# Building the token table on chip, and moving the next batch's convolution ahead

## The reference

```python
x = _layernorm(x + attention(x))                  # chunked linear attention, 16 heads, rotary, decay per head
x = _layernorm(x + selective_scan(ctx, z=x))      # per token: state = state * exp(dt * A) + dt * u * B ; y = sum(state * C)
x = _layernorm(x + experts(x))                    # 64 experts, top 8 per token, capacity 256
```

```python
probs = softmax(x @ router_weight.T)              # 2048 tokens, 64 experts
topw, topi = top_k(probs, 8);  topw /= sum(topw)
pos = (cumsum(one_hot(topi.reshape(-1))) at the chosen expert) - 1
xe[expert, pos] = x[token]   where pos < 256      # the rest is dropped
y = sum over the 8 choices of topw * expert(xe)[expert, pos]
```

## Time and profile before

| | us |
|---|---|
| median of 3 runs (1345.42 to 1348.79) | 1347.47 |
| the profiled execution | 1349.46 |
| its span, first to last instruction | 1347.6 |

### The profile page before, as it was taken

One profiled execution on the slowest core, in us unless ns is written; L12 is line 12 of the kernel. 1 busy time (PEld: TensorE's weight loads), 2 busy tenths in 40 slices (PEclk: granted clock), 3 DMA queues, 4 the chain that ended last, 5 costly groups with the idle time before them and its releaser, 6 DMA issues. The chain is left out here.

```text
span 1347.6 us, 19321 instructions
## 1 busy us (share of the span) xinstructions
PE 1138.9 (85%) x6389; PEld 757.4 (56%) x6389; DVE 1100.1 (82%) x1536; ACT 853.8 (63%) x1536; POOL 1003.9 (74%) x796
## 2 busy tenths in 40 slices
PE   7489997898979779967887718999999999999950
PEld 2234443354424434433443418999999999999940
DVE  2379988989968799878798566998888989898846
ACT  5474585734756444847345326888878888888843
POOL 0778768777899997999988744777777777777644
PEclk9698887997889789878978658999999999999985
DMA  6525425323242432163133306999999999999978
GB/s 244 140 72 191 110 65 145 99 70 83 49 111 61 124 84 51 46 154 106 38 83 102 98 13 208 302 315 305 308 304 306 305 313 301 313 301 311 285 138 326
DMA packets 97490, 235.26 MB, mean 175 GB/s; under 512 B 20704, under 2 KB 21216, under 8 KB 96752
## 3 DMA queue, kind: packets, MB, share of 16 engines
q1 hardware_dynamic: 65648, 162.66, 39.5%
q0 software_dynamic: 31744, 71.37, 22.3%
HBM read 147.48 MB, written 52.94 MB: 149 GB/s over the span
## 5 line engine op out<-in xcount | busy, mean ns | idle before, releaser
L1226 DVE TENSOR_TENSOR_SCAN hst<-hst,dbu 128x512 f32<-128x512 f32 x256 | 299.2, 1214 | 97.1 <-POOL dbu L1035 71.8
L1035 POOL TENSOR_TENSOR dbu<-rep,bc 128x1024 f32<-128x1024 f32 x128 | 301.8, 2360 | 64.1 <-PE y_ps L396 35.3
L1642 POOL DMA_INDIRECT sum_rows<-ye,tokens x128 | 205.5, 1606 | 98.4 <-ACT ye L1721 75.6
L396 PE MATMUL y_ps<-dbu,cs 128*32 128x512 f32 x512 | 167.8, 741 | 70.3 <-DVE dbu L1232 62.6
L799 ACT ACTIVATE hst<-rep,small_sb 128x512 f32<-128x512 f32 x256 | 165.9, 685 | 56.8 <-DVE dbu L1232 51.5
L1634 POOL DMA_INDIRECT xe<-x_rows,tokens x128 | 150.6, 1176 | 61.4 <-issue 37.8
L434 PE MATMUL ring<-first_raw,xT 128*128 128x512 f32 x384 | 176.7, 604 | 0.5 <-DVE x2T L1314 0.5
L1232 DVE TENSOR_TENSOR dbu<-hst,bc 128x1024 f32<-128x1024 f32 x128 | 156.7, 1224 | 4.4
L1684 PE MATMUL low<-xh,w1h 128*128 128x256 f32 x512 | 150.5, 294 | 0.0
L1684 PE MATMUL low<-xh,w1l 128*128 128x256 f32 x512 | 145.3, 284 | 0.0
L1684 PE MATMUL low<-xl,w1h 128*128 128x256 f32 x512 | 145.2, 284 | 0.0
(11 more groups left out here) (198 smaller groups left out, 2680.0 us busy)
## 6 DMA issues: line engine op xcount, KB each, us to landing
first_raw<-in_gate_up SPq DMA_DIRECT2D x64, 768.0 KB, 9.8
rep<-made SPq DMA_DIRECT2D x256, 128.0 KB
second_raw<-in_down SPq DMA_DIRECT2D x64, 256.0 KB, 5.1
bc<-bc_rows SPq DMA_DIRECT2D x64, 128.0 KB, 3.2
second_raw<-in_down SPq DMA_DIRECT2D x64, 128.0 KB, 7.2
rows<-sum_rows SPq DMA_DIRECT2D x16, 512.0 KB, 8.9
sum_rows<-x2T SPq DMA_DIRECT2D x1, 4608.0 KB, 17.2
xT<-in_x_turned SPq DMA_DIRECT2D x16, 256.0 KB, 3.0
```

Of the source, the lines that this page charges most:

```text
L396: ins = pe.matmul(y_ps[rows, :], sel, dbu[:, n % WORK, g, :], start=(k == 0), stop=(k == QUADS - 1))
L1035: pool.tensor_tensor(dbu[:, n % WORK, :, :], rep[:, i % 2, :, 1, :], bc[:, k, 0, :].unsqueeze(1).broadcast_to([P, 2, T]), ALU.mult).then_i ...
L1226: dve.tensor_tensor_scan(h, h, dbu[:, n % WORK, i, :], 0.0, ALU.mult, ALU.add).then_inc(scanned, 1)
L1642: pool.indirect_dma_start(sum_dram[e % SUMS], bass.IndirectOffsetOnAxis(ap=tokens[:, e, j:j + 1], axis=0), ye[:, e % YE, j, :], None, comp ...
```

## The change

The DRAM table, POOL's scatters, and batch 3's split into 16 x 16 go. Instead every batch has its slot numbers split into a row 0 to 127 (`slot >> 7`) and a column 0 to 127 (`slot & 127`), by `number_slots`. For 128 tokens (a pair r, j: batch and quarter) DVE makes two one-hots of 128 x 8 columns in f16, one for the rows and one for the columns (`make_hots`), ACT multiplies the second by the token's number plus one (`number_lows`), PE multiplies them in eight matmuls, one for each of the eight choices (`place_tokens`), and DVE adds the 128 x 128 result to the table in SBUF (`add_slots`). The first three batches do that in the loop, at the slots of `HOTS`: one-hots at slot n, numbering and matmuls two slots later, the addition three slots later. The counter that the one-hots are compared with is read with a step of zero in the loop (`count16`), and from a written-out copy (`count8`) for the last batch. That one follows behind the loop (`place_last`), which then fills empty slots with spare row numbers and writes `tokens`; this is before the change of block.

```diff
+HOT_AT = ((0, 3, 1), (0, 3, 4), (1, 0, 1), (1, 0, 4))
+HOT_LAST = ((0, 2, 1), (0, 2, 4), (0, 3, 0), (0, 3, 3))
+HOTS = {SLOT_COUNT * (r + 1 + over) + UNIT * c + k: (r, j)
+        for r in range(B - 1) for j, (over, c, k) in enumerate(HOT_LAST if r == B - 2 else HOT_AT)}
+def hots_due(n, later=0):
+    return (HOTS[n - later],) if n - later in HOTS else ()
+def hot_place(j):
+    return 1 if j < 2 else 0
...
+        hot = acc[...].bitcast(F16).rearrange("p (i h s k) -> p i h s k", i=2, h=2, k=TOPK)
+        hot_last = bc[...].bitcast(F16).rearrange("p (j h s k) -> p j h s k", j=NT, h=2, k=TOPK)
+        count8 = xT[:, 0, :, :]...bitcast(F16).rearrange("p (s k) -> p s k", k=TOPK)
...
+            def place_tokens(r, j):                                             # PE
+                pe.wait_ge(lows_numbered, NT * r + j + 1)
+                ps = to_fill(pe, f"slots{r}_{j}")
+                for k in range(TOPK):
+                    ins = pe.matmul(ps[:, 0:P], hot[:, hot_place(j), 1, :, k], hot[:, hot_place(j), 0, :, k],
+                                    start=(k == 0), stop=(k == TOPK - 1))
+                ins.then_inc(fill_sem(f"slots{r}_{j}"), 1)
...
+            def number_lows(r, j, lows):                                        # ACT
+                act.wait_ge(hots_made, NT * r + j + 1)
+                act.activation(lows, lows, ACT.Copy, scale=cs[:, C_TOK + NT * r + j:C_TOK + NT * r + j + 1])\
+                    .then_inc(lows_numbered, 1)
...
-            def scatter(b, first, end):                                         # POOL
-                for n in range(min(first, NT * TOPK), min(end, NT * TOPK)):
-                    pool.indirect_dma_start(table_dram, ... idx_s[:, n:n + 1] ..., tok_i[...], None)
...
-            def tell_slots(b, own):                                             # DVE
+            def number_slots(b, own):
                 own.settle()
+                own.step(dve.tensor_scalar(slot_i[:, 0, :, :], idxf[:, :, :], float(P - 1), None, ALU.add))
+                own.settle()
+                own.step(dve.tensor_scalar(slot_i[:, 1, :, :], slot_i[:, 0, :, :], 7, None, ALU.arith_shift_right))
+                own.step(dve.tensor_scalar(slot_i[:, 2, :, :], slot_i[:, 0, :, :], P - 1, None, ALU.bitwise_and))
+                own.settle()
+                own.step(dve.tensor_scalar(place_of[:, 0, :, :], slot_i[:, 1, :, :], -1.0, None, ALU.add))
+                dve.tensor_copy(place_of[:, 1, :, :], slot_i[:, 2, :, :]).then_inc(placed, 1)
+            def add_slots(r, j):
+                use = f"slots{r}_{j}"
+                ps = full(dve, use)
+                dve.tensor_tensor(tokens_f, ps[:, 0:P].rearrange("p (e j) -> p e j", j=CJ), tokens_f, ALU.add)\
+                    .then_inc(drain_sem(use), 1)
+            def make_hots(r, j, hots, count):
+                dve.wait_ge(placed, r + 1)
+                for h in range(2):
+                    ins = dve.tensor_tensor(hots[:, h, :, :], place_of[:, h, j, :].unsqueeze(1).broadcast_to([P, P, TOPK]),
+                                            count, ALU.is_equal)
+                ins.then_inc(hots_made, 1)
+            def number_tokens(r, j):
+                ...                                 # waits until the place in acc is free
+                make_hots(r, j, hot[:, hot_place(j)], count16[:, :].unsqueeze(2).broadcast_to([P, P, TOPK]))
+            def place_last(own):
+                for j in range(NT):
+                    make_hots(B - 1, j, hot_last[:, j], count8)
+                ps = full(dve, f"slots{B - 1}")
+                ...                                 # add, find empty slots, write tokens: three passes
```

The orders of the engines change with it. A line here names the place of a piece before and after (c, k as above; "k" is the slot behind whose decays, product or scan it stands):

```diff
 DVE   convolve(b + 1, 0..3)                 -c 2, k 2, 3, 4, 5            +c 2, k 0, 1, 2, 3
 PE    project_context(b + 1, 0..3)          -c 2, k 0, 1, 2, 3            +c 1, k 7 and c 2, k 0, 1, 2
 PE    project_u(b + 1)                      -c 2, k 6                     +c 2, k 5
 PE    turn_rows(b - 1, 0..1)                -in rate_experts              +ahead of update_state, mix_values
 PE    count_places(b - 1)                   -c 1, k 4                     +c 1, k 5
 ACT   first_tap(b + 1, 0..3)                -c 2, k 3, 4, 5, 6            +c 2, k 1, 2, 3, 4
 ACT   gate_u(b + 1)                         -c 2, k 7                     +c 2, k 5
 ACT   take(xdbl), soften, exponentials      -c 3, k 1, 2, 3               +c 2, k 7; c 3, k 1, 2
 ACT   logs(b + 1, EARLY)                    -c 3, k 4, with the rounding  +c 3, k 3; rounded: c 3, k 4
 ACT   logs(b, LATE)                         -c 0, k 6, with the rounding  +c 0, k 6; rounded: c 0, k 7
 ACT   exponents(b - 1)                      -c 1, k 5                     +c 1, k 4
 ACT   take_rows(b - 1, 0..3)                -c 1, k 3, 3, 4, 4            +c 1, k 2, 2, 3, 4
 ACT   gate_z(b, 2)                          -c 3, k 2                     +next batch's c 0, k 2 (last batch as before)
 ACT   excess, steps (b, 2..3)               -c 0, k 7 and c 1, k 3        +c 1, k 1 to 4
 POOL  soft_parts, soft_rest(b + 1, 0)       -c 3, k 4, 5                  +c 3, k 3, 4
 POOL  steps_of_u(b + 1, 0)                  -c 3, k 6, before inputs      +c 3, k 5, before rotate
 POOL  soft_rest(b + 1, 1)                   -c 3, k 7                     +next batch's c 0, k 0
 POOL  soft_parts(b, 2..3)                   -c 0, k 6, 7                  +c 0, k 7; c 1, k 0
 POOL  soft_parts(0, 1) before the loop      -before steps_of_u(0, 0)      +behind rotate(0)
 SP    load_context(b + 1)                   -c 1, k 6                     +c 1, k 4
 SP    store_rows(b + 1)                     -c 3, k 1                     +c 3, k 0
```

More of the change, by code:

```diff
@@ L802, in first_tap @@
             def first_tap(b, m):
-                if m == 0:
-                    wait(act, routed, b - 1)
+                if b >= 3 and m < 2:
+                    full(act, f"slots{b - 3}_{NT - 1}")
                 if m == 0 and b == 0:
@@ L818, in soften @@
             def soften(b, tiles):
+                if tiles == LATE and b >= 2:
+                    full(act, f"slots{b - 2}_1")
                 for m in tiles:
@@ L919, in _ @@
                     decays(n + 1)
+                    for r, j in hots_due(n + 1, 2):
+                        number_lows(r, j, hot[:, hot_place(j), 1, :, :])
+                    if front:
+                        first_tap(b + 1, 0)
                     if soft:
-                        act.wait_ge(bc_stored, 16 * (b + 1))
-                        take(f"xdbl{b + 1}", xdbl[:, :])
+                        soften(b + 1, EARLY)
+                    if c == 0 and b:
+                        excess(b, 1)
+                        steps(b, 1)
+                    if c == 1:
+                        excess(b, 2)
                     if back and c == 1:
@@ L927, in _ @@
                     decays(n + 2)
+                    for r, j in hots_due(n + 2, 2):
+                        number_lows(r, j, hot[:, hot_place(j), 1, :, :])
+                    if front:
+                        first_tap(b + 1, 1)
                     if soft:
-                        soften(b + 1, EARLY)
+                        exponentials(b + 1, EARLY)
                     if t:
@@ L936, in _ @@
                         gate_z(b, 1)
-                    if c == 3:
+                    if c == 3 and last:
                         gate_z(b, 2)
-                    decays(n + 3)
-                    if front:
-                        first_tap(b + 1, 0)
-                    if soft:
-                        exponentials(b + 1, EARLY)
-                    if c == 1:
-                        for m in LATE:
-                            steps(b, m)
-                    take_mixed(t)
                     if back and c == 1:
@@ L1158, in _ @@
                         n = SLOT_COUNT * b + UNIT * c + k
-                        if c == NT - 1 and k == 6 and not last:
-                            steps_of_u(b + 1, 0)
                         if n + 1 < SLOT_COUNT * B:
@@ L1194, in _ @@
-                        if k == 5 and t + 1 < NT * B:
-                            rotate(t + 1)
-                        if k in (6, 7) and c == 0:
-                            soft_parts(b, k - 4)
+                        if k == 0 and c == 0 and b:
+                            soft_rest(b, 1)
+                            steps_of_u(b, 1)
+                        if k == 7 and c == 0:
+                            soft_parts(b, 2)
+                        if k == 0 and c == 1:
+                            soft_parts(b, 3)
```

414 lines of the change are left out of this document (194 added, 220 removed).

## The result

The kernel after the change takes 1379.68 us (median of 4 runs, 1377.47 to 1381.78) against 1346.73 us for the kernel before (4 runs): the ratio is 1.0243, 95% interval 1.0221 to 1.0265. It is 2.4% slower. The forecast was 1331 us, faster. The profiled execution of the kernel after is 1381.78 us long, its span 1379.5, 2.1 us above the median.

A forecast was written before the change was run, and what follows sets the result against it. VectorE was taken to bound the loop (busy 607.14 of 704.30 us). From the profiled 1349.5 us, loop -8.6 and join -7.7 gave 1333.2; less 2.0 for the profile against the median: 1331 us, range 1315 to 1349.

The forecast's parts named there:

- scatters leave GpSimd: Loop: the 96 indirect stores leave GpSimd, and the time they cost goes: -22 us.
- the rounding: Loop, chunk 0: ScalarE's rounding passes come after the next decays, so decay stalls shrink: -1.5 us in each of four batches.
- the join: After the loop, from the places to the first gather: 24.1 us before the change, -7.7 us in sum.
- both lie two slots behind the one-hots: Loop: ScalarE's numbering (1.1 us) and TensorE's eight matmuls (1.0 us) run beside scans and cost nothing.
- If that cover is gone: Loop: should numbering and matmuls not be hidden beside scans, the price is 1.1 us twelve times, 13.
- The convolution's passes move: Loop, chunk 2: passes go from slots 2-5 to 0-3, costing 0, or 1.5 us a batch if accompanying work is late.
- the contention: Loop: VectorE's one-hots and GpSimd's instructions hinder each other: +10 us, 0.4 us per one-hot.
- Rival A: Loop: one-hots wait for GpSimd and hold up its next product, 1.6 us each: 1359 us in all; chance 0.12.
- the cover: Loop, mostly chunk 3: one-hots and additions fit into waits that VectorE already has: -13 us.
- the exponentials' wait: Loop, routing: ScalarE's exponentials come one slot sooner, and VectorE's wait for them goes: -7.5 us over three batches.
- the reordered prologue: Before the loop: `steps_of_u` comes ahead of `soft_parts`, which leaves the way of the load of `wo`: -1.6 us.
- Rival B: Loop: the waits only move, so the moves' 14.5 us are lost: 1345.5 us, no change; chance 0.12.

The follow-up runs named there:

- a_no_place: Kernel after, with TensorE's placing matmuls and VectorE's additions of the first three batches left out, one-hots and numbering kept: 1349.70 us.
- a_k_major: Kernel after, with the loop's one-hots laid out choice by choice, so that the placing matmuls read neighbouring words: 1371.21 us.
- a_spaced: Kernel after, with the one-hots that share a buffer five slots apart instead of three: 1375.38 us.
- best2: Kernel after with convolution back, dense counter, first two batches' one-hots in the last batch, the third's in the join, placing ahead of state sums: 1325.81 us.
- a_conv_back: Kernel after, with the next batch's convolution and all that follows it put back to the slots of the kernel before: 1366.02 us.
- a_between: Kernel after, with each pair of loop one-hots between the slot's two scans and its product instead of behind that product: 1377.69 us.
- a_no_loop_table: Kernel after, with no one-hots, numbering, matmuls or additions for the first three batches inside the loop: 1315.02 us.
- b_no_scatters: Kernel before, with the indirect stores of the first three batches' tokens left out: 1326.69 us.
- a_dense: Kernel after, with the loop's one-hots compared against a counter repeated eight times, dense in 16 bits: 1365.56 us.

## Why the prediction was wrong

The loop was forecast to fall by 8.6 us and rose by 38.8. In the forecast VectorE had 42.5 us more to do and 51.1 less to wait for; it had 46.9 more to do, nearly as said, and 8.1 less to wait for. Leaving out its first chunk, as in the table, it rose by 41.7. The experiments split this into four steps, each the difference of two kernels:

| step | forecast us | measured us |
|---|---|---|
| scatters leave GpSimd | -22 | -23.3 |
| the moves in the loop and `number_slots` | -11.5 | +0.1 |
| one-hots, contention, cover | +24.5 | +34.6 |
| placing and additions | +3.5 | +30.3 |

(Moves: -7.5 - 4.5 - 1 + 1.5; one-hots: 27.5 + 10 - 13. The prologue's -1.6 and the rounding's 1.5 in the first chunk lie ahead of this stretch. By these terms the forecast for it was -5.5. Taken by the ratios, which hold the join and the prologue too, the first, third and last step come out as -25.4, +32.0 and +33.9.)

- *Failed: "both lie two slots behind the one-hots, beside scans, and I cost them at nothing."* This is the largest error, 27 us. I priced TensorE's eight matmuls by their length (1.0 us; they took 2.06) and asked what they lie beside, not what stands ahead of them in an in-order queue, nor who waits for them. The buffer reuse three slots later and the addition behind the third slot are waits that the change adds, and I named no price for either: the 13 us for the case "If that cover is gone" are one numbering of 1.1 us, twelve times. The last sentence of the prediction looked for the failure at another place: "TensorE waits for the numbered one-hots and the score masks come late". TensorE never waited for them (0.0 us idle before L552), and the masks' waits fell; it was VectorE that waited for TensorE. No rival had that. a_no_place, a_k_major, a_spaced and best2 show it from four sides. Not separated is what the clock adds: TensorE's 384 projections of L434 are busy 176.7 us before, 187.0 after, 183.5 in a_no_place and 176.4 in best2, with the same code.
- *Failed: "The convolution's passes move ... 0 for all, and 1.5 us a batch if one is late."* It costs 13.6 us, 4.5 a batch. Rightly I saw that the chunk could gain nothing (VectorE 42.5 of 44.0 busy); I did not ask what it could lose. Three projections moved into the slots in which the three banks go round between scores and masks, and each came to VectorE through TensorE, ScalarE and a bank; the small projection came to VectorE through ScalarE's decays. a_conv_back shows the cost, and VectorE's waits split it: 5.6 us less for the tap, 5.9 less for the decays. That the banks are the reason for the late tap is read from the timeline and not tried by itself.
- *Mis-sized: the contention, +10.* The 24 one-hots were busy 48.2 us for 37.5 forecast, and 29.1 alone (24 x 1.211): 0.8 us each, not 0.4. The mechanism was as described, and by a_between GpSimd pays where VectorE comes first. "many one-hots start with GpSimd idle" was wrong for slot 1 of a chunk, where GpSimd's product is released by TensorE's late state sum, at the moment the pair starts. Rival A priced contention alone: its point of decision, 1.1 us each, was not reached.
- *Nearly right: the cover, -13.* In a_no_place the 24 one-hots are 45.1 us of VectorE's time and cost 34.6: 10.5 us are covered.
- *Right: the exponentials' wait goes* (7.5 to 0), but not its worth: VectorE is 1.5 us busier in each chunk 1 of a_no_loop_table, and the chunks are only 0.2 to 0.7 us shorter than in b_no_scatters. Two short passes account for it: those that write `chose` and `prev` take 1.27 and 0.90 us beside a GpSimd product in batch 2, 0.29 and 0.23 in b_no_scatters. *Right, as far as it was tried: the rounding.* For 1.5 us forecast, chunk 0 gained 2.6 in a_no_loop_table and 1.6 in best2, where the convolution stands as before (42.2 to 40.6). Other small moves fall into the same chunk.
- *Not settled: the reordered prologue, -1.6.* The profile after begins its loop 2.7 us later, but others with the same prologue begin between 50.8 and 53.8. Prologue and first chunk together did gain: the eleven kernels with the new order reach chunk 1 at 90.0 to 95.2 us, the two with the old at 95.5 and 99.4. How much of it is the prologue was not tried.
- *Right: the join.* 16.1 us from the places to the gather, 8.0 less than before, for 7.7 forecast. The last eight one-hots took 4.9 us, not the 6.9 of my middle: the Trainium skill's "VectorE: DVE Perf Modes", "What auto-detection actually checks", was right: 685 ns with every operand 16-bit and dense in its innermost step, 1211 with the counter's step of zero; a_dense agrees in the loop (677 at the shortest).

Rival B (the waits only move) has the moves' sum, +0.1, but not how it came about: chunks 0 and 3 did get 14.0 us shorter, and the convolution took 14.2 back in chunk 2. That the 14.0 is near the forecast's 13.0 for the moves is luck, since the exponentials gave 1.6 of their 7.5 and chunk 3 gave 6.2 of which the forecast had 1.3. Its 1345.5 us holds no term for TensorE. None of the four cases held 1380. The range ended at 1349 because the prices beside my costs at nothing were small: 13 us where the placing took 27 more than forecast, and 1.5 us a batch where the convolution took 4.5.

## What to carry to other kernels

A small operation added to an in-order queue can cost what stands ahead of it, each time an engine waits for it: before costing it at nothing, follow its consumer back through the queue, and give each new wait (a buffer used again, a bank taken in turn) a price of its own. Work moved ahead can collide with what shares its buffers even if the engine it runs on loses nothing: look for a stretch in which the rotating banks are free, not only for one in which the engine is. And put new work into a wait that already exists on the engine that binds, at a place where its producers and consumers idle as well. With the same table and the same count of one-hots the kernel after is 33 us slower than the kernel before and best2 is 24 faster; the new places, the convolution's return (13.6 us by a_conv_back) and the dense counter share in that.

## What the runs showed of the hardware

- A `TENSOR_TENSOR` of VectorE with both inputs in SBUF and a GpSimd `TENSOR_TENSOR` do not run together: whichever starts second waits for the end of the first (3.44 us for a pair of 1.37; 3.20 us for a product of 2.35; the longest one-hot of the kernel after 3.38 us, for 1.21 alone). The Trainium skill says so in "SBUF — State Buffer", "Who interferes with whom": with two SBUF inputs VectorE contends with GpSimd's reads, and issue order decides who blocks. The traces agree. My sum had a price for VectorE's side alone. In the kernel after VectorE's one-hots are busy 19.1 us above their length alone, and GpSimd is busy 13.1 us more in the loop than in a_no_loop_table (523.5 and 510.4).
- A VectorE `TENSOR_SCALAR` with one tile as input waited likewise: the pass that writes `chose` (128x256) in a_no_loop_table, batch 2, began at 460.88 beside a product that ended at 461.99 and took 1.27 us, 0.29 in b_no_scatters with GpSimd idle.
- A scatter beside such a pass did no harm: VectorE's `prev` pass of batch 2 takes 0.22 us in the kernel before while an indirect DMA is issued on GpSimd, as in b_no_scatters, and 0.90 us in a_no_loop_table beside a product.
- TensorE's 128x128 f16 matmuls take 416 ns with operands 16 bytes apart and 220 ns with neighbouring ones, eight of them 2.06 and 0.62 us. In a_spaced the eight take 2.06 us at a granted clock of 1.00 (376.6) as well as of 0.50 (405.3).
- A f16 comparison over 1024 columns takes 1211 ns with a broadcast operand and 677 to 685 ns with dense ones, 0.53 us less. In the loop the mean fell by 0.61 (2047 to 1436); what contention adds to each hardly shrank, from 0.84 to 0.76 us.
